# Tile norms' last steps and inverse roots on GpSimd instead of VectorE and ScalarE, in the second layer of a perceiver

## The chip, the cores and the metric

One core of a Trainium2 chip. The time is that of one whole execution on the device, in microseconds; lower is better. Engines are called TensorE (PE in the rows; PEld is its weight load), VectorE (DVE), ScalarE (ACT), GpSimd (POOL) and SyncE (SP). Each works through its own queue in program order and waits on semaphores.

## The reference

Two layers on latents x of 16 x 64 x 256 and a context of 16 x 1024 x 256. Each layer is cross-attention, then self-attention, then a feed-forward block, each behind a layer norm without weights and with a residual:

```python
def _layernorm(x, axis=-1, eps=1e-05):
    m = jnp.mean(x, axis=axis, keepdims=True)
    v = jnp.var(x, axis=axis, keepdims=True)
    return (x - m) / jnp.sqrt(v + eps)

x = x + _L1_xattn_ref(_layernorm(x, axis=-1), ctx_1024, ctx_1024, Wq, bq, Wk, bk, Wv, bv, Wo, bo)
x = x + _L1_attn_ref(_layernorm(x, axis=-1), Wq, Wk, Wv, W_O)
x = x + _L1_ffn_ref(_layernorm(x, axis=-1), w_gate, w_up, w_down)
```

The feed-forward block rounds its input to blockwise fp4, which are the steps that the change calls x steps:

```python
scale = jnp.max(jnp.abs(xb), axis=-1, keepdims=True) / 6.0
scale = jnp.maximum(scale, jnp.float32(1e-12))
xn = xb / scale
idx = jnp.searchsorted(_MID, jnp.abs(xn))
q = _GRID[idx] * jnp.sign(xn) * scale
```

## The kernel before

Everything is float32 and the order on each engine is written out by hand. The latents are 8 tiles of 128 rows (two batches) by 256. The first layer, its attention and its feed-forward block are not touched. The second layer (`second_layer`) is one program: a loop of 64 steps s, four for each of 16 batches, does the cross-attention, and the causal attention and the feed-forward block of finished tiles are woven into it. A tile is finished every 8 steps; `tile_at(s, lag)` says which tile has its turn in step s at a lag, and in this text the *place* of a step is (s - 10) mod 8, so that lag 12 falls at place 4 and lag 14 at place 6.

In a step the cross-attention does: TensorE `scores` (L722), in even steps `times_v` (L749) of a finished pair, `project_v` two steps ahead (L681), `transposes` of the step before in two halves (L732) and in between `project_k` four steps ahead (L667), unless that batch's keys were made early (batches 0, 4, 8, 12, 13 and 14: steps 12 to 15, 28 to 31 and 44 to 55 have no key projection, nor have the last four). VectorE takes two row maxima of 128x1024 (L859), an inverse of a row sum (L892), v out of its bank (L841), the transposed probabilities of one half (L869), the second inverse. ScalarE does two exponentials (L802) and takes the other half (L813) and the keys (L772). GpSimd multiplies the two halves of probabilities with the inverses (`normalise`, L655, 128x1024 each), twice in eight steps spreads the queries (L638), and for the causal attention does `spread_queries` (L1908, place 4) and `distances` (L1915, place 6). TensorE's results go round over banks 4 to 7, so TensorE waits for VectorE or ScalarE to empty a bank before it fills the next.

A tile norm (`TileNorm`; norm1 in front of the causal attention, tiles `ca_sn_*`; norm2 in front of the feed-forward block, tiles `ca_fn_*`) has four parts: statistics and variance on VectorE (L1698 to L1702; norm1 at place 0, norm2 at place 2), the root on ScalarE (L1706; norm1 at place 1, norm2 at place 4), and on VectorE a reciprocal, one Newton step (L1710 to L1717) and the 128x256 result (L1719; norm1 at place 2, norm2 at place 6). Square root and exponential are in different activation tables, so a table load stands before the root and one before the exponential after it. TensorE transposes norm1's result at place 3 (L1761), behind `project_v` and in front of that step's `transposes`.

Norm2's result goes through the x steps of the feed-forward input on VectorE: scale and division at place 6 (L173 to L176 on `ca_ff_x`), rounding at place 7 (L178 to L181 and L2069; scratch in `wi_gateT`). TensorE transposes it at place 0 (L1983). Behind the loop stands the tail (from 1299 us): the last two causal tiles and the feed-forward block's matmuls of all tiles (L1993, L2015), with rounding of the hidden values on VectorE and GpSimd. The norms of tile 7 (both) and 6 (norm2) fall in the tail, and so do the x steps of tiles 5 to 7.

## Time and profile before

| | us |
|---|---|
| three timed runs, median (lowest to highest) | 1418.12 (1415.79 to 1420.81) |
| the profiled execution | 1421.31 |
| its span, first to last instruction | 1418.0 |
| busy: TensorE matmuls | 1294.1 (91%) |
| busy: VectorE | 976.0 (69%) |
| busy: ScalarE | 802.0 (57%) |
| busy: GpSimd | 690.7 (49%) |

The profile is of one execution. A matmul's end is modelled, so TensorE can be shown as busy while it waits inside a group; how long a step takes is the surer figure. Idle time in brackets is that of the engine just before the instruction, with what ended it. The granted clock is TensorE's, 1.0 for 2.4 GHz and 0.5 for 1.2 GHz. An average over the span says little here, since the stages have different limits; what is to be read are the steps of the second layer's loop, from 725.8 to 1299 us.

### The profile page before, as it was taken

Reading aid. Unit: us, or ns where it says so; the run is one execution under the profiler, and the core shown is the slowest. Engines: PE = TensorE matmul, PEld = TensorE weight load, DVE = VectorE, ACT = ScalarE, POOL = GpSimd, SP = SyncE. Lnnn points to the kernel's source line nnn. Section 1 sums busy time; section 2 is a strip of 40 time slices with the busy share of each in tenths; the row PEclk is TensorE's granted clock in tenths of the full one; section 3 lists DMA queues with packets and bytes.
Section 4 is the critical chain, followed back from the end, with each engine's and each line's share of the span. In section 5 each row is a group of like instructions: output and inputs, shape, how many; then the busy total and the mean of one; then the engine's idle time right before and its main releaser. Section 6 shows DMA issues by size and latency. Waiting matters only on the chain. (4 is left out here: it accounts for less than half of the span.)

```text
span 1418.0 us, 28592 instructions
## 1 busy us (share of the span) xinstructions
PE 1294.1 (91%) x11120; PEld 899.6 (63%) x11122; DVE 976.0 (69%) x1876; ACT 802.0 (57%) x1373; POOL 690.7 (49%) x383
## 2 busy tenths in 40 slices
PE   6999999999999988988789999998998988888887
PEld 3666666667667665546456676666665676666564
DVE  4685776766666654856777767688766879776674
ACT  4766666666666655536456656556465645565431
POOL 2856656566666542310146654444445455544333
PEclk9999999999999999999999999999899989999999
DMA  5312112112113030007330210020010121000000
GB/s 164 101 51 66 46 46 67 46 60 76 46 46 113 2 113 1 1 5 219 106 93 31 60 52 31 31 61 31 31 51 31 44 61 47 31 2 1 5 9 18
DMA packets 30533, 74.23 MB, mean 52 GB/s; under 512 B 4033, under 2 KB 16193, under 8 KB 26177
## 3 DMA queue, kind: packets, MB, share of 16 engines
q1 hardware_dynamic: 30400, 72.41, 16.8%
q8 instruction: 90, 1.47, 0.4%
q14 instruction: 43, 0.34, 0.1%
HBM read 65.06 MB, written 7.34 MB: 51 GB/s over the span
## 5 line engine op out<-in xcount | busy, mean ns | idle before, releaser
L655 POOL TENSOR_TENSOR ca_prob<-ca_prob,ca_inv_sum 128x1024 f32<-128x1024 f32 x256 | 493.6, 1935 | 448.5 <-DVE ca_inv_sum L892 448.4
L732 PEld LDWEIGHTS bank<-ident,ca_prob 128*128 128x128 f32 x2048 | 240.9, 143 | 102.5 <-issue 75.2
L732 PE MATMUL bank<-ident,ca_prob 128*128 128x128 f32 x2048 | 273.7, 278 | 29.2 <-DVE ca_v L841 25.4
L856 DVE CUSTOM_DVE_ANT_0 ca_neg_logit<-bank,ca_mask_add 128x1024 f32<-128x1024 f32 x128 | 151.6, 1221 | 103.7 <-PE bank L722 76.6
L802 ACT ACTIVATE ca_prob<-bank,ca_neg_max 128x1024 f32<-128x1024 f32 x128 | 142.3, 1113 | 110.7 <-DVE ca_neg_max L859 110.5
L859 DVE TENSOR_REDUCE ca_neg_max<-bank 128x1 f32<-128x1024 f32 x128 | 150.5, 1218 | 59.9 <-PE bank L722 59.6
L802 ACT ACTIVATE ca_prob<-ca_neg_logit,ca_neg_max 128x1024 f32<-128x1024 f32 x128 | 146.9, 1149 | 68.3 <-DVE ca_neg_max L856 68.3
L869 DVE COPY ca_probT<-bank 128x512 f32<-128x512 f32 x256 | 163.7, 681 | 7.0 <-PE bank L732 7.0
L813 ACT ACTIVATE ca_probT<-bank 128x512 f32<-128x512 f32 x256 | 139.6, 594 | 50.8 <-PE bank L732 48.5
L722 PE MATMUL bank<-ca_kT,ca_q_blk 32*128 32x512 f32 x1024 | 150.3, 657 | 4.5 <-DVE ca_v L841 2.7
L749 PEld LDWEIGHTS bank<-ca_probT,ca_v 128*32 128x32 f32 x4096 | 111.8, 113 | 55.7 <-issue 42.4
L772 ACT ACTIVATE ca_kT<-bank,ca_bk 64x512 f32<-64x512 f32 x128 | 87.3, 682 | 104.1 <-PE bank L667 103.2
L749 PE MATMUL bank<-ca_probT,ca_v 128*32 128x128 f32 x4096 | 129.5, 280 | 4.9 <-issue 4.0
L667 PE MATMUL bank<-ca_ctxT,ca_wk 128*128 128x512 f32 x256 | 121.8, 601 | 10.1 <-DMA ca_bk<-in_L_xattn_bk 9.1
L681 PE MATMUL bank<-wv,ctxT 128*128 128x256 f32 x512 | 127.3, 392 | 0.0
L681 PE MATMUL bank<-ca_wv,ca_ctxT 128*128 128x256 f32 x512 | 127.3, 392 | 0.0
L681 PEld LDWEIGHTS bank<-ca_wv,ca_ctxT 128*128 128x128 f32 x512 | 92.3, 190 | 41.1 <-issue 28.2
L681 PEld LDWEIGHTS bank<-wv,ctxT 128*128 128x128 f32 x512 | 92.3, 190 | 41.2 <-issue 31.2
L772 ACT ACTIVATE ca_kT<-bank,ek_bk 64x512 f32<-64x512 f32 x80 | 54.6, 682 | 77.0 <-PE bank L667 76.3
L667 PE MATMUL bank<-ctxT,ek_wk 128*128 128x512 f32 x160 | 79.5, 624 | 4.4 <-DVE ca_v L841 2.4
L667 PEld LDWEIGHTS bank<-ca_ctxT,ca_wk 128*128 128x128 f32 x256 | 44.6, 193 | 43.6 <-issue 33.3
L892 DVE RECIPROCAL ca_inv_sum<-ca_row_sum 128x1 f32<-128x1 f32 x256 | 40.6, 159 | 41.6 <-ACT ca_prob L802 34.4
(281 smaller groups left out, 1712.2 us busy)
## 6 DMA issues: line engine op xcount, KB each, us to landing
ca_ctxT<-in_ctxT SPq DMA_DIRECT2D x16, 1024.0 KB, 5.3
ctxT<-in_ctxT SPq DMA_DIRECT2D x16, 1024.0 KB, 4.8
ca_mask_i<-in_mask SPq DMA_DIRECT2D x32, 256.0 KB, 6.1
ek_ctxT<-in_ctxT SPq DMA_DIRECT2D x12, 512.0 KB, 5.3
early_k<-ek_out SPq DMA_DIRECT2D x48, 128.0 KB, 3.4
ca_kT<-early_k SPq DMA_DIRECT2D x12, 512.0 KB, 5.7
...
```

The source lines that it names most:

```text
L655: pool.tensor_tensor(self.prob[:, x, :], self.prob[:, x, :], self.inv_sum[:, x:x + 1].broadcast_to([P, CTX]), ALU.mult).then_inc(self.norm ...
L667: mm = pe.matmul(self.core.bank[:, x, :], self.wk[:, k, m * P:(m + 1) * P], self.ctxT[:, b % 2, k, half * HALF_CTX:(half + 1) * HALF_CTX], ...
L681: mm = pe.matmul(self.core.bank[:, x, r * D:(r + 1) * D], self.ctxT[:, b % 2, k, ch * P:(ch + 1) * P], self.wv[:, k, :], start=(k == 0), s ...
L722: mm = pe.matmul(self.core.bank[:, 2 * j + half, :], self.q_blk[rows, b % 2, u, :, :], self.kT[rows, b % 2, u, :], start=True, stop=True, ...
L732: tr = pe.transpose(self.core.bank[:, x, n * P:(n + 1) * P], self.prob[:, 2 * (s % 2) + p, (4 * h + n) * P:(4 * h + n + 1) * P], self.core ...
L749: mm = pe.matmul(self.core.bank[32 * j:32 * j + 32, x, 0:P], self.v[:, b % 2, ch, m * P + 32 * j:m * P + 32 * j + 32], self.probT[:, n % 2 ...
L772: op = act.activation(self.kT[half * S:(half + 1) * S, b % 2, 2 * m + r, :], self.core.bank[r * S:(r + 1) * S, x, :], ACT.Identity, bias=s ...
L802: act.activation(self.prob[:, y, :], source, ACT.Exp, bias=self.neg_max[:, y:y + 1], scale=-1.0 if self.masked else 1.0, accum_out=self.ro ...
L813: self.banks.free(act.activation(self.probT[:, n % 2, 4 * h:4 * h + 4, 2 * (s % 2) + p, :], self.core.bank[:, x, :].rearrange("p (n q) -> ...
L856: dve.tensor_tensor_reduce(self.neg_logit[:, p, :], scores, self.mask_add[:, b % 2, :], -1.0, BIG, ALU.add, ALU.min, self.neg_max[:, y:y + ...
L859: dve.tensor_reduce(self.neg_max[:, y:y + 1], scores, AX.X, ALU.max, negate=True).then_inc(self.max_ready, 1)
L869: self.banks.free(dve.tensor_copy(self.probT[:, n % 2, 4 * h:4 * h + 4, 2 * (s % 2) + p, :], self.core.bank[:, x, :].rearrange("p (n q) -> ...
```

## The change

The square root on ScalarE is gone from the tile norms. VectorE makes a first guess of 1/sqrt(var) from the bits of the float (`first_guess`, two operations of 128x1), and three Newton steps of four 128x1 operations each (`improve`) make it exact enough. For the 7 first norms and the 6 second norms in the loop `improve` and the two 128x256 operations behind it (`finish_on_pool`: subtract the mean, multiply by the inverse root) run on GpSimd, norm1 at place 2 and norm2 at place 5, both behind that step's `normalise`. Norm2 was finished at place 6 before. In the tail, `improve` runs on VectorE.

Of the x steps, VectorE keeps the scale (0 to 2) at place 6 and one of the rounding operations (4) at place 7. GpSimd does the division (3, place 6), three operations at place 7 (5 to 7; the former `scalar_tensor_tensor` is a `tensor_scalar` and a `tensor_tensor`) and two at place 0 (8 and 9). TensorE transposes the result at place 1 instead of 0, and ScalarE takes it there. Statistics of a tile now wait until the norm of the tile before is finished. In the tail, TensorE's `times_v(30)` comes in front of the first gate projection, VectorE copies the last probabilities before it turns to the hidden values, and the x steps of tile 5 are shared with GpSimd.

```diff
+GUESS = 0x5F3759DF
 class TileNorm:
+    STEPS = 14
     def stats_on_vector(self, dve, t):
+        wait(dve, self.xn_ready, t)
...
-    def root_on_scalar(self, act, t):
-        act.wait_ge(self.var_ready, t + 1)
-        act.activation(self.std[:, :], self.var[:, :], ACT.Sqrt).then_inc(self.std_ready, 1)
+    def first_guess(self, dve, t):
+        bits = self.rstd[:, :].bitcast(I32)
+        dve.wait_ge(self.var_ready, t + 1)
+        dve.tensor_scalar(bits, self.var[:, :].bitcast(I32), 1, None, ALU.logical_shift_right).then_inc(self.fix_step, 1)
+        dve.wait_ge(self.fix_step, self.STEPS * t + 1)
+        dve.tensor_scalar(bits, bits, -1, GUESS, ALU.mult, ALU.add).then_inc(self.fix_step, 1)
+
+    def improve(self, eng, t):
+        done, n0 = self.fix_step, self.STEPS * t + 2
+        for n in range(n0, n0 + 12, 4):
+            eng.wait_ge(done, n)
+            eng.tensor_tensor(self.fix[:, :], self.rstd[:, :], self.rstd[:, :], ALU.mult).then_inc(done, 1)
+            eng.wait_ge(done, n + 1)
+            eng.tensor_tensor(self.fix[:, :], self.fix[:, :], self.var[:, :], ALU.mult).then_inc(done, 1)
+            eng.wait_ge(done, n + 2)
+            eng.tensor_scalar(self.fix[:, :], self.fix[:, :], -0.5, 1.5, ALU.mult, ALU.add).then_inc(done, 1)
+            eng.wait_ge(done, n + 3)
+            eng.tensor_tensor(self.rstd[:, :], self.rstd[:, :], self.fix[:, :], ALU.mult).then_inc(done, 1)
+        eng.wait_ge(done, n0 + 12)
+
+    def finish_on_pool(self, pool, t):
+        lat, wide = self.core.lat[:, t, :], [P, D]
+        self.improve(pool, t)
+        pool.tensor_tensor(self.xn[:, :], lat, self.mv[:, 0:1].broadcast_to(wide), ALU.subtract).then_inc(self.centred, 1)
+        pool.wait_ge(self.centred, t + 1)
+        pool.tensor_tensor(self.xn[:, :], self.xn[:, :], self.rstd[:, 0:1].broadcast_to(wide), ALU.mult)\
+            .then_inc(self.xn_ready, 1)
...
         @block.tensor
...
-                for t in tile_at(s, 16):
+                for t in tile_at(s, 17):
                     ff.latent_transposes(pe, t)
...
+            ca.times_v(pe, 30)
             ff.project(pe, 0, 0)
-            ca.times_v(pe, 30)
...
         @block.gpsimd
...
                 for t in tile_at(s, 6):
                     sa.distances(pool, t)
+                for t in tile_at(s, 2):
+                    causal_input(t)
+                for t in tile_at(s, 13):
+                    feed_forward_input(t)
+                for t in tile_at(s, 14):
+                    ff.x_step_on(pool, t, 3, 4)
+                for t in tile_at(s, 15):
+                    ff.x_step_on(pool, t, 5, 8)
+                for t in tile_at(s, 16):
+                    ff.x_step_on(pool, t, 8, 10)
...
         @block.vector
...
                 for t in tile_at(s, 2):
-                    causal_input(t)
+                    norm1.first_guess(dve, t)
+                for t in tile_at(s, 13):
+                    norm2.first_guess(dve, t)
...
                 for t in tile_at(s, 14):
-                    feed_forward_input(t)
+                    ff.scale_x(dve, t, norm2.xn_ready)
                 for t in tile_at(s, 15):
-                    ff.round_x(dve, t)
+                    ff.x_step_on(dve, t, 4, 5)
...
             ca.take_pv(dve, 30)
-            feed_forward_input(5)
+            ff.scale_x(dve, 5, norm2.xn_ready)
+            ca.take_t_on_vector(dve, STEPS - 1, 0)
             ff.hidden(dve, 0)
-            ff.round_x(dve, 5)
-            ca.take_t_on_vector(dve, STEPS - 1, 0)
             ff.round_hidden(dve, 0)
```

ScalarE's queue at the first norm of tile 0 (place 1 to 3; `ca_sn_std` is the root), one piece of the difference:

```order
 L813 ACTIVATE ca_probT<-bank 128x4x128 x2
-L1706 ACT_TABLE_LOAD
-L1706 ACTIVATE ca_sn_std<-ca_sn_var 128x1
-L802 ACT_TABLE_LOAD
 L802 ACTIVATE ca_prob,ca_row_sum<-bank,ca_neg_max 128x1024 x2
 L813 ACTIVATE ca_probT<-bank 128x4x128 x2
```

The root and both table loads are gone; the exponentials follow the copies at once. There are 634 rows of ScalarE before and 587 now.

VectorE's queue at places 6 and 7 of one tile, before (from the second inverse of place 6 to the maxima of the step behind place 7; `wi_gateT` is scratch):

```order
L892 RECIPROCAL ca_inv_sum<-ca_row_sum 128x1
L1710 RECIPROCAL ca_fn_rstd<-ca_fn_std 128x1
L1712 SCALAR_TENSOR_TENSOR ca_fn_fix<-ca_fn_rstd,ca_fn_var 128x1
L1715 TENSOR_SCALAR ca_fn_fix<-ca_fn_fix 128x1
L1717 TENSOR_TENSOR ca_fn_rstd<-ca_fn_rstd,ca_fn_fix 128x1
L1719 TENSOR_SCALAR ca_ff_x<-lat,ca_fn_mv,ca_fn_rstd 128x256
L173 TENSOR_REDUCE ca_ff_xmag<-ca_ff_x 128x16
L174 TENSOR_SCALAR ca_ff_xscale<-ca_ff_xmag 128x16
L175 RECIPROCAL ca_ff_xinv<-ca_ff_xscale 128x16
L176 TENSOR_TENSOR ca_ff_x<-ca_ff_x,ca_ff_xinv 128x256
L859 TENSOR_REDUCE ca_neg_max<-bank 128x1 x2
```

and now, of another tile:

```order
L892 RECIPROCAL ca_inv_sum<-ca_row_sum 128x1
L173 TENSOR_REDUCE ca_ff_xmag<-ca_ff_x 128x16
L174 TENSOR_SCALAR ca_ff_xscale<-ca_ff_xmag 128x16
L175 RECIPROCAL ca_ff_xinv<-ca_ff_xscale 128x16
L859 TENSOR_REDUCE ca_neg_max<-bank 128x1 x2
```

Six of the nine operations between the second inverse of place 6 and the next step's maxima have left VectorE.

GpSimd's queue from place 4 to place 7 of one tile, before:

```order
L1908 TENSOR_TENSOR ek_ctxT<-ek_ctxT,small 128x1024
L655 TENSOR_TENSOR ca_prob<-ca_prob,ca_inv_sum 128x1024 x4
L1915 TENSOR_TENSOR ek_out<-ek_out,ca_sa_top 128x1024
L655 TENSOR_TENSOR ca_prob<-ca_prob,ca_inv_sum 128x1024 x4
L638 TENSOR_TENSOR ca_q_blk<-ca_q,small 128x512
```

and now (two more rounds of the four 128x1 operations are left out):

```order
L655 TENSOR_TENSOR ca_prob<-ca_prob,ca_inv_sum 128x1024 x2
L1723 TENSOR_TENSOR ca_fn_fix<-ca_fn_rstd 128x1
L1725 TENSOR_TENSOR ca_fn_fix<-ca_fn_fix,ca_fn_var 128x1
L1727 TENSOR_SCALAR ca_fn_fix<-ca_fn_fix 128x1
L1729 TENSOR_TENSOR ca_fn_rstd<-ca_fn_rstd,ca_fn_fix 128x1
...
L1735 TENSOR_TENSOR ca_ff_x<-lat,ca_fn_mv 128x256
L1737 TENSOR_TENSOR ca_ff_x<-ca_ff_x,ca_fn_rstd 128x256
L655 TENSOR_TENSOR ca_prob<-ca_prob,ca_inv_sum 128x1024 x2
L1938 TENSOR_TENSOR ek_out<-ek_out,ca_sa_top 128x1024
L176 TENSOR_TENSOR ca_ff_x<-ca_ff_x,ca_ff_xinv 128x256
```

Between the products of place 5 and those of place 6 there now stand 14 operations, and the division stands behind the distances. At place 2 the same 14 stand on `ca_sn_*` and `ek_ctxT`. GpSimd has 188 rows in all before and 421 now.

## Rows read from the trace of the kernel before

**Rows 1.** windows, first without norm, then place 6: us; each engine's busy us; PEclk

```profile
776.52:784.86 8.34, 8.34 (x101) 5.96 (x97) 6.62 (x10) 4.78 (x10) 5.09 (x3) 1.00 0.01 2
...
1082.58:1094.13 11.55, 11.55 (x118) 8.66 (x115) 10.43 (x18) 5.34 (x10) 5.65 (x3) 1.00 0.09 13
...
sum 66.64, PE 64.89 PEld 49.21 DVE 58.75 ACT 28.43 POOL 33.32; mean PE 10.81 PEld 8.20 DVE 9.79 ACT 4.74 POOL 5.55
```

**Rows 2.** windows of place 5: without root, with one, and the sum of six

```profile
833.15:841.39 8.24, 7.40 (x88) 5.92 (x92) 6.82 (x10) 3.42 (x6) 7.22 (x5) 1.00 0.28 89
903.12:917.90 14.78, 11.96 (x73) 8.12 (x76) 6.90 (x10) 8.09 (x13) 7.48 (x5) 0.77 0.01 2
...
sum 68.98, PE 55.63 PEld 40.75 DVE 41.28 ACT 36.21 POOL 47.49; mean PE 9.27 PEld 6.79 DVE 6.88 ACT 6.04 POOL 7.92
```

**Rows 3.** windows of places 7 and 0: before feed-forward input, and sum of six

```profile
849.23:867.35 18.12, 17.89 (x213) 12.53 (x214) 12.20 (x22) 12.74 (x23) 9.85 (x6) 1.00 0.17 60
...
sum 116.22, PE 102.23 PEld 68.25 DVE 84.84 ACT 73.46 POOL 51.78; mean PE 17.04 PEld 11.38 DVE 14.14 ACT 12.24 POOL 8.63
```

**Rows 4.** timeline of ScalarE in step 39: start us, us, instruction

```profile
1069.99 1.28 ACT L1706 ACT_TABLE_LOAD   x1
...
1071.51 1.28 ACT L802 ACT_TABLE_LOAD   x1
```

**Rows 5.** timeline of TensorE in steps 39 to 41; in brackets idle before

```profile
1074.96 2.00 PE L1792 MATMUL bank<-ek_ctxT 64*128 64x64 f32 x32 [2.83 <-DVE ca_v L841]
1076.89 3.66 PE L667 MATMUL bank<-ctxT,ek_wk 128*128 128x512 f32 x4
...
1087.04 1.88 PE L667 MATMUL bank<-ctxT,ek_wk 128*128 128x512 f32 x4
...
1089.72 1.14 PE L722 MATMUL bank<-ca_kT,ca_q_blk 32*128 32x512 f32 x8
...
1092.62 1.04 PE L732 MATMUL bank<-ident,ca_prob 128*128 128x128 f32 x8
```

**Rows 6.** timeline of VectorE in step 40

```profile
1088.48 1.89 DVE L1712 SCALAR_TENSOR_TENSOR ca_fn_fix<-ca_fn_rstd,ca_fn_var 128x1 f32<-128x1 f32 x1
...
1090.60 1.64 DVE L1717 TENSOR_TENSOR ca_fn_rstd<-ca_fn_rstd,ca_fn_fix 128x1 f32<-128x1 f32 x1
...
1094.13 2.35 DVE L859 TENSOR_REDUCE ca_neg_max<-bank 128x1 f32<-128x1024 f32 x2
```

**Rows 7.** timeline of GpSimd in step 40

```profile
1085.33 1.89 POOL L655 TENSOR_TENSOR ca_prob<-ca_prob,ca_inv_sum 128x1024 f32<-128x1024 f32 x1 [7.27 <-DVE ca_inv_sum L892]
1088.47 1.89 POOL L655 TENSOR_TENSOR ca_prob<-ca_prob,ca_inv_sum 128x1024 f32<-128x1024 f32 x1 [1.25 <-DVE ca_inv_sum L892]
1090.32 1.90 POOL L1915 TENSOR_TENSOR ek_out<-ek_out,ca_sa_top 128x1024 f32<-128x1024 f32 x1
```

**Rows 8.** timeline of TensorE in steps 13, 36 and 37

```profile
820.32 1.46 PE L732 MATMUL bank<-ident,ca_prob 128*128 128x128 f32 x8 [1.95 <-DVE ca_v L841]
...
1046.44 2.00 PE L1843 MATMUL bank<-ek_ctxT 64*64 64x256 f32 x16 [0.85 <-DVE ca_attnT L883]
...
1054.07 0.38 PE L1761 MATMUL bank<-ident,ek_ctxT 128*128 128x128 f32 x2
```

**Rows 9.** timeline of GpSimd at the start and in step 36

```profile
0.24 0.10 POOL L2544 MEMSET const-float32-0.0<- 128x1 f32 x1 [0.24 <-issue]
...
1048.24 1.89 POOL L655 TENSOR_TENSOR ca_prob<-ca_prob,ca_inv_sum 128x1024 f32<-128x1024 f32 x1 [0.52 <-DVE ca_inv_sum L892]
```

**Rows 10.** groups of GpSimd by form: count, busy us, mean ns, idle before

```profile
L638 POOL TENSOR_TENSOR ca_q_blk<-ca_q,small 128x512 f32<-128x512 f32 x32 | 33.2, 1038 | 43.0 <-DVE ca_q L832 43.0
```

**Rows 11.** timeline of TensorE in the tail

```profile
1316.84 3.64 PE L749 MATMUL bank<-ca_probT,ca_v 128*32 128x128 f32 x64 [4.04 <-issue]
...
1387.54 0.61 PE L1983 MATMUL bank<-ident,ca_ff_x 128*128 128x128 f32 x2 [2.92 <-DVE ca_ff_x L2069]
```

More of the change, by code:

```diff
@@ L2043, in take_hidden, with x_free, x_step_on, scale_x @@
                         ("fh", t, 1))
-    def x_free(self, dve, t):
+    def x_free(self, eng, t):
         if t >= 1:
-            self.banks.wait_filled(dve, ("fx", t - 1))
-    def x_steps(self):
-        return fp4_steps(self.x[:, :], DB, self.xmag[:, :], self.xscale[:, :], self.xinv[:, :], self.x[:, :],
-                         self.xe)
-    def divide_x(self, dve, t, xn_ready):
-        dve.wait_ge(xn_ready, t + 1)
-        steps = self.x_steps()
-        for n in range(4):
-            steps[n](dve).then_inc(self.x_step, 1)
-            dve.wait_ge(self.x_step, 8 * t + n + 1)
-    def round_x(self, dve, t):
-        steps = self.x_steps()
-        for n in range(4, 8):
-            steps[n](dve).then_inc(self.x_step, 1)
-            dve.wait_ge(self.x_step, 8 * t + n + 1)
-        grid, scale = fp4_scaled(self.x[:, :], self.xscale[:, :], DB)
-        dve.tensor_tensor(grid, grid, scale, ALU.mult).then_inc(self.x_ready, 1)
+            self.banks.wait_filled(eng, ("fx", t - 1))
+    def x_step_on(self, eng, t, first, last):
+        x, e = self.x[:, :], self.xe
+        steps = fp4_steps(x, DB, self.xmag[:, :], self.xscale[:, :], self.xinv[:, :], x, e)
+        grid, scale = fp4_scaled(x, self.xscale[:, :], DB)
+        for n in range(first, last):
+            wait(eng, self.x_step, 9 * t + n)
+            if n < 6:
+                steps[n](eng).then_inc(self.x_step, 1)
+            elif n == 6:
+                eng.tensor_scalar(x, x, 1.0 - 2.0**-24, None, ALU.mult).then_inc(self.x_step, 1)
+            elif n == 7:
+                eng.tensor_tensor(x, x, e, ALU.add).then_inc(self.x_step, 1)
+            elif n == 8:
+                steps[7](eng).then_inc(self.x_step, 1)
+            else:
+                eng.tensor_tensor(grid, grid, scale, ALU.mult).then_inc(self.x_ready, 1)
+    def scale_x(self, dve, t, xn_ready):
+        dve.wait_ge(xn_ready, t + 1)
+        self.x_step_on(dve, t, 0, 3)
     def h_steps(self, t):
@@ L2320, in _ @@
                     sa.take_heads(act, t)
-                for t in tile_at(s, 16):
+                for t in tile_at(s, 17):
                     ff.take_latents(act, t)
@@ L2331, in _ @@
                     ca.take_q_on_scalar(act, 1)
-                for t in tile_at(s, 1):
-                    norm1.root_on_scalar(act, t)
                 for t in tile_at(s, 3):
@@ L2338, in _ @@
                     sa.take_transposed(act, t)
-                for t in tile_at(s, 12):
-                    norm2.root_on_scalar(act, t)
             ff.silu(act, 0)
@@ L2443, in _ @@
             ff.round_hidden(dve, 1)
-            causal_input(7)
+            norm1.first_guess(dve, 7)
+            banks.wait_filled(dve, ("sx", 6))
+            norm1.finish_on_vector(dve, 7)
             ff.hidden(dve, 2)
@@ L2455, in _ @@
             ff.hidden(dve, 4)
-            ff.round_x(dve, 6)
+            ff.x_step_on(dve, 6, 4, 10)
             sa.divide(dve, 7)
```

41 lines of the change are left out of this document (19 added, 22 removed).

## The prediction

> **What bounds the kernel now.** I read the windows first, one for each step of the second layer's cross-attention loop (64 steps, from 725.8 to 1299 us of the span; a step begins with VectorE's first row maximum), because the change touches this loop and the tail behind it and nothing before them. Then I read who waits inside the long steps.
>
> The loop repeats every 8 steps with one latent tile. Step s has place (s - 10) mod 8. At place 6, a step without any norm takes 8.34 us and TensorE is busy in all of it; the same TensorE work takes 11.55 as soon as VectorE also has the last steps of the second norm in it, and VectorE is then busy for 10.43 [rows 1]. Place 5 takes up to 14.78 us with a second norm's root in front of it and 8.24 without [rows 2]. Places 7 and 0 together take 18.12 us before there is feed-forward input, and (116.22 - 18.12) / 5 = 19.6 on average in the next five pairs [rows 3]. So the loop is TensorE's by nature, and some 8 to 10 us in every 8 steps go to other engines at three places.
>
> What they are is seen in one tile. *Place 5, ScalarE:* the root costs two table loads of 1.28 us, the second charged to the next exponential, which so can't begin before 1072.79 [rows 4]; without them it could begin with its maximum, at about 1070.6. VectorE's take of v comes behind its inverse, and so behind that exponential; TensorE waits 2.83 us for it, and then the granted clock falls: the key projection takes 3.66 us there and 1.88 in the next step [rows 5], and the mean clock of the worst step at this place is 0.77 [rows 2], a mix of the 2.4 and the 1.2 GHz level. *Place 6, VectorE:* a 128x1 operation with two SBUF inputs takes 1.89 us, exactly until GpSimd's 128x1024 multiply ends, and the next such takes 1.64, until GpSimd's next operation ends [rows 6, 7]. The scores of step 41 are complete at 1090.86 [rows 5] and their maximum starts at 1094.13 [rows 6].
>
> **The change part by part.** All sums are made against the profiled execution: 1421.3 us with a span of 1418.0, 3.2 above the median of the three timed runs (1418.1).
>
> *1. Place 6, norm off VectorE.* Five long steps, 66.64 - 8.34 = 58.3 us [rows 1]. From the end of the second blocked operation to the maximum there are 1.9 us (1092.24 to 1094.13 [rows 6]) for five operations, three of which stay: under 1.2 us, and the short step leaves VectorE 8.34 - 6.62 = 1.7 [rows 1]. Four steps go to 8.34. The fifth, step 48, has no key projection and is bound by VectorE: I put it at 8.1. New sum 41.5, gain **16.8**.
>
> *2. Place 5, no table loads.* Five steps, 68.98 - 8.24 = 60.7 us [rows 2]. The 8.24 us step has no key projection, like three of the five; with 0.35 for two new 128x1 operations (first_guess) those come to 8.6. The other two have one: 8.24 less the 0.84 that TensorE was idle in it, plus 1.88 [rows 2, 5], is 9.3; since part of those 8.24 was VectorE's, I take 9.0. New sum 43.8, gain 16.9. If the idle went but the low clock stayed, only the wait would be won, some 2.3 us in each, 11.5 in all. Step 63 has the same stall in front of the tail: 1.5 more. Together **18.4**.
>
> *3. Places 7 and 0.* 98.1 us in five pairs [rows 3]. VectorE keeps one of five rounding operations, and TensorE no longer starts place 7 behind a late maximum. At 18.12 each the sum is 90.6; one pair has no key projections and may get 2 more. Gain **9.5**, between nothing and that.
>
> *4. Places 2 and 3, the first norm.* Its table loads end in a wait of TensorE, 0.85 us in front of the causal output [rows 8], seven tiles: 6.0. Against it stands a new latency: GpSimd does 12 operations of 128x1 and two of 128x256 behind its normalise. Their price is in no row. From 128x512 in 1.04 [rows 10] and 128x1024 in 1.89 [rows 7] the fixed part is 1.04 - 0.85 = 0.19, and a memset of 128x1 takes 0.10 [rows 9]. Between 0.10 and 1.04 I take 0.25 with the hand-over, nearest to the fixed part: 12 x 0.25 = 3.0. A 128x256 is 0.19 + 0.43 = 0.62, two are 1.3. So x is ready 4.3 us behind the normalise. TensorE left 3.9 in step 36 (1050.13 to 1054.07 [rows 8, 9]): short by 0.4. In the four tiles without key projections TensorE comes 1.9 sooner: short by 2.3, but there it waited 1.95 just behind these transposes [rows 8]. At worst 3 x 0.4 + 4 x 2.3 = 10.4 lost; with that wait and an exponential that starts sooner I take 3. Net **3**.
>
> *5. What GpSimd's queue does to others.* Behind the 4.3 us stands the next step's normalise. At place 5 GpSimd has 3.8 + 4.3 = 8.1 of 8.6 us; but TensorE reads the product only in the step after: one normalise ends at 1087.2 [rows 7], its transposes start at 1092.6 [rows 5], 5 us later, and a delay of 1 to 2 hides in that. Places 6, 7 and 0 get about 0.6, 2.4 and 1.4 us more. I cost it at nothing; the cover is that slack, and beyond it each microsecond costs one per step. VectorE loses a little: at place 7 its one rounding operation may meet a busy GpSimd for up to 1.9 us, five times, mostly in slack: **-2.5**.
>
> The page "SBUF — State Buffer" of the Trainium skill (Who interferes with whom) says that a VectorE operation with two SBUF inputs and a GpSimd operation that reads SBUF exclude each other for a whole instruction; the 1.89 and 1.64 above agree. By it everything moved to GpSimd is one more thing to wait for, but what stays of the norms on VectorE in the loop has one SBUF input, so it leaves the sum as it is.
>
> *6. The tail.* TensorE waits 4.04 us in front of the last times_v [rows 11], for copies that VectorE makes behind the rounding of x(5); the new order puts the copy first and the rounding on GpSimd: -4. The norms of tiles 7, 6 and 7 stay on VectorE, with 14 small operations instead of 4; at about 0.19 each 10 more cost 1.9, part of which lies in waits like those of rows 6. The last stands in front of a wait of TensorE, 2.92 us for x(7) [rows 11], and costs its full 1.9 with the one more rounding operation; the two others together 1. Net -4 + 2.9: a gain of **1**, between 6 and -3.
>
> Sum: 16.8 + 18.4 + 9.5 + 3 - 2.5 + 1 = 46 us. 1421.3 - 46 = 1375, and as a median 3 below that: **1372 us**.
>
> **The rivals.**
>
> *GpSimd's small operations are dear (the other side).* Place: the 14 GpSimd operations between the normalise and TensorE's transposes of x at place 3, which in TensorE's order stand before everything else of that step. Each 0.1 us above 0.25 adds 1.2 us to seven first norms, 8.4 in all. Above about 0.5 the second norm fills place 5 too (3.8 + 6 + 1.3 over 8.6), 12 us per tile for each further microsecond. At 0.5: 21 us lost, 1393. The gain is used up at about 0.7; at 0.75 the first norms lose 12 x 0.5 x 7 = 42 and the second 12 x 0.25 x 6 = 18, 60 against 46 won: 1432. Against it: the fixed part of 0.19. For it: no row shows a 128x1 arithmetic operation on GpSimd. The page "GPSIMD Engine Reference" of the Trainium skill (Performance versus the Vector engine) keeps elementwise work on VectorE, with 1.96 times its time for an addition of 2048 elements; that speaks against the change only where GpSimd becomes the bound, and no row here shows that.
>
> *The low clock moves with the idle.* TensorE idles some 2 us in front of x at place 3 in four tiles, and the half-clock stretches stay. Then term 2 keeps 11.5 of 16.9, term 3 about 3 of 9.5, and term 4 is -1: 46 - 15.9 = 30 us, 1388.
>
> *More than forecast.* VectorE doesn't bound the steps without key projection, which drop by up to 1.9 at five places, and the tail gives 6: 46 + 9 + 5 = 60 us, 1358.
>
> *The waits were hidden anyway,* and something that I don't see sets the step: 1418. Against it: 8.34 against 11.55 us at equal TensorE work.
>
> **How the numbers follow.** Forecast (1362 to 1382) 0.50; more than that 0.15; low clock stays, or small operations at 0.4 to 0.5 (1382 to 1400) 0.25; dear operations short of break-even 0.05; no change 0.02; slower 0.03. The range leaves out the far end of the 0.15 and the last three: 1354 to 1398. Faster by over 0.3% (about what a measurement of this kernel can tell) 0.95, within it 0.02, slower by over 0.3% 0.03.
>
> **What would show it.** Step 40 at 8.3 to 8.5 us, step 39 at about 9; no table load between the first step and the tail; GpSimd's 128x1 operations 0.25 us from start to start; TensorE's idle in front of the transposes of x at place 3 under 1 us with key projection and 2 to 3 without; the granted clock 1.0 at places 5 and 7. The forecast is wrong if the 128x1 operations take 0.5 or more, or if TensorE waits for a normalise that stands behind them.

## The result

The changed kernel takes 1378.74 us (median of 4 runs, 1377.42 to 1384.67), the kernel before 1416.95 beside it (1411.2 to 1420.81): ratio 0.9742, 95% interval 0.9697 to 0.9786, some 37 us less. The forecast was 1372 in 1354 to 1398. The profiled executions took 1377.42 and 1421.31 us, with spans of 1375.6 and 1418.0. The first is the fastest of the changed kernel's four and the second slower than all four of the other's, so the differences between the two traces add up to 42.4 us, some 5 more than the ratio gives. Of the other kernels below, only the profiled execution of roots ran at a lower mean clock than its timed ones (0.923 against 0.975; 1429.31 us), so only its times are used.

The head of the page of the changed kernel: VectorE and ScalarE are each busy for some 40 us less, GpSimd for 74 more, with 601 instructions where the kernel before had 383 (the counts under The change are of merged rows).

```profile
span 1375.6 us, 28748 instructions
PE 1270.7 (92%) x11120; PEld 881.9 (64%) x11122; DVE 935.1 (68%) x1839; ACT 759.8 (55%) x1326; POOL 764.6 (56%) x601
```

The loop of the second layer, up to the first maximum of its last step 63, went from 566.6 to 521.5 us; what is left, step 63 and the tail, from 125.6 to 129.2. TensorE's mean granted clock rose from 0.95 to 0.99 in the first stretch and was 0.90 and 0.89 in the second. Windows of the changed kernel (columns as in [rows 1]): place 6 without norm, then with one and the sum of six, against [rows 1]; place 5 in step 31 and the sum, against [rows 2]; places 7 and 0, the sum, against [rows 3].

```profile
775.66:784.00 8.34, 8.34 (x101) 5.96 (x97) 6.62 (x10) 4.78 (x10) 5.09 (x3) 1.00 0.00 0
1057.95:1066.30 8.35, 8.35 (x101) 5.96 (x97) 7.21 (x13) 4.79 (x10) 5.82 (x7) 1.00 0.01 2
sum 49.66, PE 49.66 PEld 36.17 DVE 42.60 ACT 26.36 POOL 39.42; mean PE 8.28 PEld 6.03 DVE 7.10 ACT 4.39 POOL 6.57
...
972.83:984.64 11.81, 8.81 (x67) 7.07 (x68) 7.10 (x13) 3.53 (x6) 10.83 (x18) 0.71 0.01 1
sum 56.75, PE 48.40 PEld 37.07 DVE 42.23 ACT 23.93 POOL 52.19; mean PE 8.07 PEld 6.18 DVE 7.04 ACT 3.99 POOL 8.70
...
sum 109.19, PE 105.51 PEld 74.09 DVE 72.71 ACT 74.69 POOL 79.64; mean PE 17.58 PEld 12.35 DVE 12.12 ACT 12.45 POOL 13.27
```

Place 6 now takes as long as a step without norm. Place 5 is shorter except in step 31, which keeps its 12 us and its low clock.

Timeline of TensorE in step 39 and GpSimd at its end (start, duration, instruction, idle before in brackets). Where TensorE waited 2.83 us and then ran at half clock [rows 5] it waits 0.69 and keeps its clock (1.98 us for the key projection), and GpSimd's 128x1 operation takes 0.19 us, 0.27 from start to start.

```profile
1052.03 2.00 PE L1815 MATMUL bank<-ek_ctxT 64*128 64x64 f32 x32 [0.69 <-DVE ca_v L841]
1053.96 1.98 PE L667 MATMUL bank<-ctxT,ek_wk 128*128 128x512 f32 x4
...
1055.08 0.19 POOL L1723 TENSOR_TENSOR ca_fn_fix<-ca_fn_rstd 128x1 f32<-128x1 f32 x1
1055.35 0.19 POOL L1725 TENSOR_TENSOR ca_fn_fix<-ca_fn_fix,ca_fn_var 128x1 f32<-128x1 f32 x1
```

In the tail small operations of the first norm of tile 7 stand still on VectorE while GpSimd works, and TensorE waits for the norm (5.40 us; before 2.5). TensorE also waits longer in front of L1866, for a causal result that VectorE makes behind the second norm of tile 6, and in front of L2006, for x(7): 4.85 us each, where it was 3.1 and 2.92 [rows 11].

```profile
1279.60 1.28 DVE L1723 TENSOR_TENSOR ca_sn_fix<-ca_sn_rstd 128x1 f32<-128x1 f32 x1
1280.92 0.16 DVE L1725 TENSOR_TENSOR ca_sn_fix<-ca_sn_fix,ca_sn_var 128x1 f32<-128x1 f32 x1
1281.11 0.15 DVE L1727 TENSOR_SCALAR ca_sn_fix<-ca_sn_fix 128x1 f32<-128x1 f32 x1
1281.30 1.04 DVE L1729 TENSOR_TENSOR ca_sn_rstd<-ca_sn_rstd,ca_sn_fix 128x1 f32<-128x1 f32 x1
...
1284.75 0.69 PE L1784 MATMUL bank<-ident,ek_ctxT 128*128 128x128 f32 x2 [5.40 <-DVE ek_ctxT L1742]
```

The same norm's operations stood still in the kernel before, too, and for as long in all (2.4 us):

```profile
1330.35 1.54 DVE L1712 SCALAR_TENSOR_TENSOR ca_sn_fix<-ca_sn_rstd,ca_sn_var 128x1 f32<-128x1 f32 x1
...
1332.10 1.24 DVE L1717 TENSOR_TENSOR ca_sn_rstd<-ca_sn_rstd,ca_sn_fix 128x1 f32<-128x1 f32 x1
```

What is new there is their number: from the first of them to the start of the 128x256 operation it is 5.13 us now and was 3.23.

### The profile page after: what moved, and what is told of

It reads as the page before. It is cut to its first block and busy times, and to the rows that moved or that the text cites. A ratio compares the mean times of both kernels' runs of the same rounds, so it can differ in the third digit from the quotient of the medians.

```text
span 1375.6 us, 28748 instructions
## 1 busy us (share of the span) xinstructions
PE 1270.7 (92%) x11120; PEld 881.9 (64%) x11122; DVE 935.1 (68%) x1839; ACT 759.8 (55%) x1326; POOL 764.6 (56%) x601
## 5 line engine op out<-in xcount | busy, mean ns | idle before, releaser
L732 PEld LDWEIGHTS bank<-ident,ca_prob 128*128 128x128 f32 x2048 | 237.2, 142 | 76.2 <-issue 53.3
L732 PE MATMUL bank<-ident,ca_prob 128*128 128x128 f32 x2048 | 267.1, 275 | 7.3 <-DVE ca_v L841 4.3
L722 PE MATMUL bank<-ca_kT,ca_q_blk 32*128 32x512 f32 x1024 | 147.2, 644 | 4.6 <-DVE ca_v L841 2.7
L749 PEld LDWEIGHTS bank<-ca_probT,ca_v 128*32 128x32 f32 x4096 | 108.7, 110 | 48.7 <-issue 33.4
L749 PE MATMUL bank<-ca_probT,ca_v 128*32 128x128 f32 x4096 | 126.0, 275 | 0.9 <-DVE ca_probT L869 0.9
L667 PE MATMUL bank<-ctxT,ek_wk 128*128 128x512 f32 x160 | 76.0, 600 | 2.6 <-PEq L100 2.1
L722 PEld LDWEIGHTS bank<-ca_kT,ca_q_blk 32*128 32x128 f32 x1024 | 40.4, 184 | 30.7 <-issue 26.0
```

The source lines that it names most:

```text
L667: mm = pe.matmul(self.core.bank[:, x, :], self.wk[:, k, m * P:(m + 1) * P], self.ctxT[:, b % 2, k, half * HALF_CTX:(half + 1) * HALF_CTX], ...
L722: mm = pe.matmul(self.core.bank[:, 2 * j + half, :], self.q_blk[rows, b % 2, u, :, :], self.kT[rows, b % 2, u, :], start=True, stop=True, ...
L732: tr = pe.transpose(self.core.bank[:, x, n * P:(n + 1) * P], self.prob[:, 2 * (s % 2) + p, (4 * h + n) * P:(4 * h + n + 1) * P], self.core ...
L749: mm = pe.matmul(self.core.bank[32 * j:32 * j + 32, x, 0:P], self.v[:, b % 2, ch, m * P + 32 * j:m * P + 32 * j + 32], self.probT[:, n % 2 ...
```

## The experiments

The change does three things at once: no square root on ScalarE, the norms' last steps on GpSimd, and the rounding of x on GpSimd. My theory was that the first pays at places 5, 2 and 3, and the second at place 6, because GpSimd makes VectorE's operations with two SBUF inputs stand still there. The rivals were that only one of the two matters, or that it is the number of VectorE's operations that counts. Ratios are to the kernel before, run on the same chip; 0.001 is 1.4 us.

| kernel | median us | ratio | 95% interval |
|---|---|---|---|
| the change | 1378.74 | 0.9742 | 0.9697 to 0.9786 |
| roots | 1397.45 | 0.9852 | 0.9815 to 0.9889 |
| root2 | 1386.44 | 0.9781 | 0.9745 to 0.9818 |
| vector_norms | 1422.28 | 1.0045 | 1.0027 to 1.0063 |
| vector_singles | 1383.11 | 0.9765 | 0.9722 to 0.9808 |
| before_singles | 1393.38 | 0.9843 | 0.9811 to 0.9875 |
| x_vector | 1391.64 | 0.9801 | 0.9752 to 0.9850 |
| pool_long1 | 1405.94 | 0.9936 | 0.9913 to 0.9960 |
| pool_singles | 1376.55 | 0.9708 | 0.9674 to 0.9742 |
| fw_late | 1377.82 | 0.9735 | 0.9707 to 0.9762 |
| swap | 1375.44 | 0.9706 | 0.9676 to 0.9736 |
| tail_singles | 1376.15 | 0.9714 | 0.9687 to 0.9741 |
| best | 1356.79 | 0.9590 | 0.9566 to 0.9615 |

### The square roots back: roots, root2

```diff
                 if s == Q_STEPS[0]:
                     ca.take_q_on_scalar(act, 1)
+                for t in tile_at(s, 1):
+                    norm1.root_on_scalar(act, t)
...
+                for t in tile_at(s, 12):
+                    norm2.root_on_scalar(act, t)
```

> The changed kernel with ScalarE's square roots back in the loop of the second layer, at their old places 1 and 4, on the same variance; nobody uses the result (only the next tile's variance waits for it). Norms and rounding stay where the change put them. Theory (the table loads are what place 5 and places 2 and 3 paid for, VectorE's blocked operations are a second cause at place 6): the exponential of place 5 is late again by 1.28 + 1.28 us, TensorE waits and the granted clock falls there; of the 12.3 us won at place 5 nearly all is lost again and of the 11.1 at places 2 and 3 about 7: 1379 + 19 = 1398 us, 1391 to 1402. Place 6 stays at 8.3 to 8.8. Rival (the gain is VectorE's relief alone, ScalarE has room for its tables): within 3 us of 1379.

Measured 1397.45, as the theory had it; where in the loop it was lost isn't shown. root2 has the second norm's root alone:

> The changed kernel with ScalarE's square root back for the second norm only, at place 4 of the loop (unused result, as in the run that brought both back). Theory (the table loads at place 5 alone carry term 2): place 5 goes from 56.8 us in its six steps back to 69, as before the change, places 2 and 3 stay: 1379 + 12 = 1391 us, 1388 to 1394; the other 7 of the 18.7 us that both roots cost belong to the first norm's. Rival (it is the first norm's root that costs): 1379 to 1384.

Measured 1386.44: 7.7 us for the second norm's root, not 12, and 18.7 - 7.7 = 11.0 for the first norm's (by the ratios 5.5 and 10). Its place 5 takes 65.9 us instead of 56.8; in step 39 the stall is what it was in [rows 4, 5], with the half clock behind it:

```profile
1055.68 1.28 ACT L802 ACT_TABLE_LOAD   x1
...
1059.13 3.68 PE L1821 MATMUL bank<-ek_ctxT 64*128 64x64 f32 x32 [2.83 <-DVE ca_v L841]
```

The roots thus cost 16 us by the ratios (19 by the medians) in the changed kernel, where nobody reads their result; what they cost the kernel before, which needs it, no run shows.

### The norms on VectorE again, in two forms: vector_norms, vector_singles

```diff
                 for t in tile_at(s, 14):
+                    norm2.first_guess(dve, t)
+                    ff.x_free(dve, t)
+                    norm2.finish_on_vector(dve, t)
                     ff.scale_x(dve, t, norm2.xn_ready)
```

(The first norm gets the same at place 2, and GpSimd keeps the second norm of tile 5 alone.)

> The changed kernel with the Newton steps and the last step of both norms on VectorE in the loop, at the places of the kernel before (tile 5's second norm, in the last step of the loop, stays on GpSimd). No table loads come back; each norm has nine 128x1 operations with two SBUF inputs on VectorE, where the kernel before had two. Theory (such an operation waits for the end of GpSimd's, up to 1.9 us each): place 6 goes from 8.3 back over 11.5 us, to 12 to 15, and place 2 gets longer too: 1379 + 5 x 4 to 5 x 7 + up to 10 = 1399 to 1424. Rival (only the table loads mattered, VectorE has 1.7 us to spare in that step): 1379 to 1384.

Measured 1422.28, 0.45% slower than the kernel before. VectorE and GpSimd in step 40:

```profile
1079.98 1.64 DVE L1723 TENSOR_TENSOR ca_fn_fix<-ca_fn_rstd 128x1 f32<-128x1 f32 x1
1081.65 1.83 DVE L1725 TENSOR_TENSOR ca_fn_fix<-ca_fn_fix,ca_fn_var 128x1 f32<-128x1 f32 x1
1083.51 0.15 DVE L1727 TENSOR_SCALAR ca_fn_fix<-ca_fn_fix 128x1 f32<-128x1 f32 x1
1083.70 0.16 DVE L1729 TENSOR_TENSOR ca_fn_rstd<-ca_fn_rstd,ca_fn_fix 128x1 f32<-128x1 f32 x1
...
1079.71 1.89 POOL L655 TENSOR_TENSOR ca_prob<-ca_prob,ca_inv_sum 128x1024 f32<-128x1024 f32 x1 [1.25 <-DVE ca_inv_sum L892]
1081.56 1.90 POOL L1938 TENSOR_TENSOR ek_out<-ek_out,ca_sa_top 128x1024 f32<-128x1024 f32 x1
```

The first two tensor_tensor operations end where GpSimd's two end (1081.6, 1083.5). From then on GpSimd is idle and the same operations take 0.16 us.

```diff
-            eng.tensor_tensor(self.fix[:, :], self.rstd[:, :], self.rstd[:, :], ALU.mult).then_inc(done, 1)
-            eng.tensor_tensor(self.fix[:, :], self.fix[:, :], self.var[:, :], ALU.mult).then_inc(done, 1)
+            eng.tensor_scalar(self.fix[:, :], self.rstd[:, :], self.rstd[:, 0:1], self.var[:, 0:1], ALU.mult,
+                              ALU.mult).then_inc(done, 1)
...
-            eng.tensor_tensor(self.rstd[:, :], self.rstd[:, :], self.fix[:, :], ALU.mult).then_inc(done, 1)
+            eng.tensor_scalar(self.rstd[:, :], self.rstd[:, :], self.fix[:, 0:1], None, ALU.mult).then_inc(done, 1)
```

> As vector_norms, but each Newton step is three tensor_scalar operations on 128x1 (the factors come in as the per-partition scalars), so none has two full SBUF inputs; 9 instead of 12 operations. Theory (it is the exclusion with GpSimd that costs, not the number of small operations): each takes about 0.1 us whatever GpSimd does, 9 x 0.1 to 9 x 0.15 = about 1.2 us per norm, inside the 1.7 us that VectorE is idle at place 6: 1376 to 1386 us, place 6 at 8.3 to 9. Rival (many small dependent operations on VectorE cost by their number): like vector_norms, over 1395.

Measured 1383.11, on the same engine and at the same places: 39 us less by the form (this includes the tail, which has the new form too, and nine operations for each norm instead of twelve). VectorE in step 40, with GpSimd busy from 1065.85 to 1069.60:

```profile
1066.87 0.27 DVE L1723 TENSOR_SCALAR ca_fn_fix<-ca_fn_rstd,ca_fn_var 128x1 f32<-128x1 f32 x1
1067.17 0.15 DVE L1726 TENSOR_SCALAR ca_fn_fix<-ca_fn_fix 128x1 f32<-128x1 f32 x1
1067.36 0.21 DVE L1728 TENSOR_SCALAR ca_fn_rstd<-ca_fn_rstd,ca_fn_fix 128x1 f32<-128x1 f32 x1
...
1068.36 1.40 DVE L1741 TENSOR_SCALAR ca_ff_x<-lat,ca_fn_mv,ca_fn_rstd 128x256 f32<-128x256 f32 x1
```

None of the nine small operations stands still. But the 128x256 one does, and place 6 takes 10.65 us, not the 8.3 to 9 that I expected.

### The form alone, in the kernel before: before_singles

```diff
-        dve.scalar_tensor_tensor(self.fix[:, :], self.rstd[:, :], self.rstd[:, 0:1], self.var[:, :], ALU.mult,
-                                 ALU.mult).then_inc(self.fix_step, 1)
+        dve.tensor_scalar(self.fix[:, :], self.rstd[:, :], self.rstd[:, 0:1], self.var[:, 0:1], ALU.mult,
+                          ALU.mult).then_inc(self.fix_step, 1)
...
-        dve.tensor_tensor(self.rstd[:, :], self.rstd[:, :], self.fix[:, :], ALU.mult).then_inc(self.fix_step, 1)
+        dve.tensor_scalar(self.rstd[:, :], self.rstd[:, :], self.fix[:, 0:1], None, ALU.mult).then_inc(self.fix_step, 1)
```

> The kernel before with two operations of each norm in another form: the 128x1 scalar_tensor_tensor and tensor_tensor of its Newton step become tensor_scalar with the factors as per-partition scalars. Same engine, same number, the square roots stay on ScalarE. Theory (the 1.89 and 1.64 us at place 6 are GpSimd's exclusion, which tensor_scalar of one element does not meet): these two drop to about 0.25 each, 3.0 us per norm; the 128x256 operations behind them are then met by GpSimd instead and give 1.2 to 1.5 back, so place 6 goes from 11.5 to about 9.9 in five steps: -8, and -3 in place 2 and the tail: 1416 - 11 = 1405, 1400 to 1409. Rival (what VectorE lacks at place 6 is time for all its operations): 1414 to 1416.

Measured 1393.38: 22 us gained where I expected 11, by two operations in another form, as many as before on the same engine. Between the two traces, 28.4 us apart, place 6 gives 6.3 us; places 2 and 3, which I had at 1 or 2, give 9.6, places 7 and 0 give 5.1, the tail 3.3. VectorE at place 6, against [rows 6]:

```profile
1074.24 0.27 DVE L1712 TENSOR_SCALAR ca_fn_fix<-ca_fn_rstd,ca_fn_var 128x1 f32<-128x1 f32 x1
1074.55 0.15 DVE L1715 TENSOR_SCALAR ca_fn_fix<-ca_fn_fix 128x1 f32<-128x1 f32 x1
1074.74 0.21 DVE L1717 TENSOR_SCALAR ca_fn_rstd<-ca_fn_rstd,ca_fn_fix 128x1 f32<-128x1 f32 x1
1074.99 1.28 DVE L1719 TENSOR_SCALAR ca_ff_x<-lat,ca_fn_mv,ca_fn_rstd 128x256 f32<-128x256 f32 x1
...
1076.76 1.30 DVE L174 TENSOR_SCALAR ca_ff_xscale<-ca_ff_xmag 128x16 f32<-128x16 f32 x1
```

22 us for the form and 16 for the roots make 38; the whole change gives 37. The first was measured in the kernel before and the second in the changed one, and no run has both with the rounding of x left on VectorE, so it isn't shown that they add up. What is shown is that moving the norms adds little once their form is right: vector_singles, with everything of the norms on VectorE, is within 5 us of the change, and 7 behind tail_singles, which shares its tail. Its rounding of x stands on GpSimd, as in the change; what that is worth comes next.

### The rounding of x on VectorE again: x_vector

```diff
                 for t in tile_at(s, 14):
                     ff.scale_x(dve, t, norm2.xn_ready)
+                    ff.x_step_on(dve, t, 3, 4)
                 for t in tile_at(s, 15):
-                    ff.x_step_on(dve, t, 4, 5)
+                    ff.x_step_on(dve, t, 4, 6)
+                    wait(dve, ff.x_step, 9 * t + 6)
+                    ff.x_both(dve)
+                    ff.x_step_on(dve, t, 8, 10)
```

(x_both is the scalar_tensor_tensor of the kernel before. GpSimd's three calls go, and TensorE and ScalarE turn to the result one step sooner.)

> The changed kernel with the rounding of the feed-forward input on VectorE in the loop, as before the change: its divide at place 6, the other five operations at place 7, TensorE's transposes of it at place 0 again in place of 1. The norms stay on GpSimd. Theory (term 3 of the sum): the 7.0 us that places 7 and 0 won are lost, place 6 gets some 1 us longer in one or two tiles, place 1 gives 2.0 back: 1379 + 5 = 1384, 1382 to 1389. Rival (VectorE has enough room without the norms; those places were won by TensorE not starting behind a late maximum): 1379 - 2 = 1377.

Measured 1391.64, 13 us more than the change by the medians and 8 by the ratios, more than expected, but not where expected. Place 1 gives its 2.0 us back (53.8 to 51.8). Place 7 loses 3.4 and place 0 wins 1.5, so places 7 and 0 lose 1.9 of the 7.0 us that I had put there; this speaks for the rival on the late maximum. The surprise is place 6, 57.5 to 66.2 in seven steps. (Place 5 takes 3.9 more with the same idle time in each step, by half clock alone; the four executions spread from 1381 to 1395.) Two operations stand still there in step 40:

```profile
1069.80 1.65 DVE L174 TENSOR_SCALAR ca_ff_xscale<-ca_ff_xmag 128x16 f32<-128x16 f32 x1
1071.49 0.25 DVE L175 RECIPROCAL ca_ff_xinv<-ca_ff_xscale 128x16 f32<-128x16 f32 x1
1071.77 1.79 DVE L176 TENSOR_TENSOR ca_ff_x<-ca_ff_x,ca_ff_xinv 128x256 f32<-128x256 f32 x1
```

In the changed kernel L174 stands still for 1.65 us as well, but it is the last that does, and the maximum is ready to start 0.25 us before its scores are there.

### What GpSimd's chain costs: pool_long1, pool_singles

```diff
-        for n in range(n0, n0 + 12, 4):
+        for n in range(n0, n0 + (self.STEPS - 2 if t < 7 else 12), 4):
```

(STEPS is 26 for the first norm and stays 14 for the second.)

> The changed kernel with six Newton steps instead of three in the first norm of tiles 0 to 6 on GpSimd (the extra steps change nothing in the result): 12 more dependent 128x1 operations at 0.26 to 0.27 us from start to start, 3.2 us. It measures what each further microsecond of this chain costs, the premise of the rival on dear operations. Theory (the chain already ends just behind what TensorE has to do in every tile, so nearly all of it shows): 7 x 3.2 = 22 us, less some slack in the three tiles with key projections: 1379 + 20 = 1399, 1396 to 1402. Rival (TensorE's work or later slack absorbs it): up to 1385.

Measured 1405.94, 27 us for 7 x 12 x 0.27 = 22.8 us more chain: 1.2 us for each. TensorE's idle in front of the transposes of x, from the line's view of the changed kernel (idle us, times):

```profile
  POOL ek_ctxT L1737: 9.3, 4
```

and of pool_long1:

```profile
  POOL ek_ctxT L1737: 32.6, 7
```

23.3 us more are idle; the rest is half clock behind it (granted clock 0.79 to 0.87 in five of the seven steps, 1.0 in all seven before). The chain was to be shortened by the new form:

> As tail_singles (which took 1376), and GpSimd's Newton steps in the loop are three tensor_scalar operations each too: 9 operations instead of 12. Theory (six Newton steps instead of three cost 30 us at place 3, 1.35 us for each of the chain): 3 x 0.27 = 0.8 us less per first norm, 7 x 0.8 to 7 x 0.8 x 1.4: 1376 - 7 = 1369, 1367 to 1372. Rival (a tensor_scalar with scalars from SBUF takes longer on GpSimd than the 0.19 us of the others, no row shows it): 1375 to 1378.

Measured 1376.55, the same as tail_singles; the rival holds. Its three operations on GpSimd (minimum/median/maximum ns) take 0.81 us together, the four of the change 0.76 with one more hand-over:

```profile
L1723 POOL TENSOR_SCALAR ca_sn_fix<-ca_sn_rstd,ca_sn_var x21: 340/341/342, 814.9 to 1239.9; 128x1 f32<-128x1 f32 x21
L1726 POOL TENSOR_SCALAR ca_sn_fix<-ca_sn_fix x21: 190/190/191, 815.3 to 1240.3; 128x1 f32<-128x1 f32 x21
L1728 POOL TENSOR_SCALAR ca_sn_rstd<-ca_sn_rstd,ca_sn_fix x21: 277/283/296, 815.6 to 1240.6; 128x1 f32<-128x1 f32 x21
```

### What is left at place 5: fw_late, swap

Step 31 was the one that won nothing. fw_late changes `FW_SCALE = (10, 31, 52)` to `(10, 32, 52)`.

> The changed kernel with GpSimd's scaling of the second feed-forward weight (2.8 us) one step later, in step 32 instead of 31. Theory (at place 5 GpSimd has normalise 3.8 + norm 4.3 + scaling 2.8 us = 10.9 in an 11.8 us step; that step alone of place 5 won nothing, 11.98 to 11.82): step 31 goes to 9.3 to 9.7 and step 32 stays near 8.3, 1379 - 2.3 = 1376.5 us. Rival (the stall of step 31 has another cause, or only moves): 1379 to 1380.

Measured 1377.82: my theory on the scaling fell. TensorE still waits 3.00 us. GpSimd, TensorE and VectorE of fw_late in steps 30 and 31:

```profile
972.14 3.33 POOL L655 TENSOR_TENSOR ca_prob<-ca_prob,ca_inv_sum 128x1024 f32<-128x1024 f32 x1 [0.52 <-DVE ca_inv_sum L892]
975.43 1.04 POOL L638 TENSOR_TENSOR ca_q_blk<-ca_q,small 128x512 f32<-128x512 f32 x1
976.43 1.89 POOL L1931 TENSOR_TENSOR ek_ctxT<-ek_ctxT,small 128x1024 f32<-128x1024 f32 x1
...
978.38 0.89 PE L1815 MATMUL bank<-ek_ctxT 64*128 64x64 f32 x12 [3.00 <-POOL ek_ctxT L1931]
...
971.98 1.74 DVE L181 TENSOR_TENSOR ca_fw_raw<-ca_fw_raw,ca_fw_e 128x1536 f32<-128x1536 f32 x1
```

This time VectorE stops GpSimd: its weight rounding started first, and GpSimd's normalise takes 3.33 us instead of 1.89. Behind it stand the next block of queries and the spread of the causal queries, for which TensorE waits. The kernel before has the same 3.33 and 3.00. swap puts the spread in front:

```diff
+                for t in tile_at(s, 4):
+                    sa.spread_queries(pool, t)
                 if s % GROUPS == 2 and s // GROUPS + 1 < B:
                     ca.queries(pool, s // GROUPS + 1)
-                for t in tile_at(s, 4):
-                    sa.spread_queries(pool, t)
```

> The changed kernel with GpSimd's spread of the causal queries (place 4) in front of its next block of cross-attention queries instead of behind it. The trace shows TensorE's causal scores at place 5 waiting for this spread in every tile (1.0 to 3.0 us, 3.0 in step 31, where VectorE's weight rounding also holds GpSimd up), while nobody needs the other block before the step's end. Theory (the stall left at place 5 is GpSimd's queue, not the norm's): each of six stalls shortens by up to 1.04 us, the half clock behind step 31's goes: 1379 - 6 = 1373, 1370 to 1376. Rival (the block of queries is needed at once, or the stall has another end): 1379 to 1382.

Measured 1375.44, 3 us less by the medians and 5 by the ratios; the intervals overlap, but the stall of step 31 is 2.00 us instead of 3.00 and place 5 takes 54.7 instead of 56.8. In steps 15, 23 and 55 the wait for the spread is gone, and one of 0.7 us for v stands there, as in step 39.

### The tail: tail_singles

The operations take the form of vector_singles, for the three norms in the tail only.

> The changed kernel, its loop untouched; in the tail alone the three norms that VectorE does there (first norm of tile 7, second of tiles 6 and 7) take each Newton step as three tensor_scalar operations instead of four operations of which three have two SBUF inputs. Theory (the tail lost 3.6 us instead of winning 1 because these small operations stand still while GpSimd works, and TensorE waits for each norm): the tail falls from 129.2 to the 118.9 us that it took in vector_singles: 1379 - 10 = 1369 us, 1366 to 1372. Rival (the tail is set by where the loop leaves it, the low clock ahead of it, and vector_singles came into it with other work done): 1379.

In the profile the tail takes 120.0 us instead of 129.2, and the first norm of tile 7, from its guess to its end, 3.3 instead of 5.5. But the profiled execution (1370.58) is the fastest of six; the median of 1376.15 is only 3 to 4 us better. The mean clock is 0.985 in that one and 0.978 to 0.981 in the others. Which stretches the other executions ran at half clock isn't recorded, so where some 5 us of the 9 went stays open.

### What the runs point to: best

All Newton steps in the new form, on VectorE, behind the guess and beside GpSimd's normalise; GpSimd keeps the two 128x256 operations.

```diff
     def finish_on_pool(self, pool, t):
         lat, wide = self.core.lat[:, t, :], [P, D]
-        self.improve(pool, t)
+        pool.wait_ge(self.fix_step, self.STEPS * (t + 1))
...
                 for t in tile_at(s, 2):
                     norm1.first_guess(dve, t)
+                    norm1.improve(dve, t)
                 for t in tile_at(s, 13):
                     norm2.first_guess(dve, t)
+                    norm2.improve(dve, t)
```

With it go swap and three moves in VectorE's tail: the first norm of tile 7 ahead of `ff.round_hidden(dve, 1)`, `sa.divide(dve, 7)` ahead of the rounding of x(6), and the rounding of x(7) ahead of `ff.round_hidden(dve, 5)`.

> What the runs so far point to, together. All Newton steps are three tensor_scalar operations, and VectorE does them, also in the loop, right behind the guess, while GpSimd is still at its normalise; GpSimd keeps the two 128x256 operations of each norm and the rounding. The spread of the causal queries stands in front of the next block of queries. In the tail the first norm of tile 7 stands in front of the rounding of hidden(1), the causal divide of tile 7 in front of the rounding of x(6), and the rounding of x(7) in front of that of hidden(5). Theory: the 12 x 0.27 = 3.2 us leave GpSimd's chain and GpSimd cannot stop them on VectorE: TensorE's idle at place 3 (0.15 to 3.44 us, 10.3 in seven tiles) nearly goes, -9, against +1 where VectorE has no room; the spread gives 3; the tail goes from 129 to 121 by the form of the operations and to 116 by its order, of which a half shows in the median if it is as with tail_singles: 1379 - 8 - 3 - 3 - 5 = 1360 us, 1354 to 1366. Rival (with 2 us more on VectorE at places 2 and 5 TensorE waits there for its maxima and the low clock returns): 1370 to 1375.

Measured 1356.79 (1354.79 to 1356.95), ratio 0.9590: 22 us better than the change, 56 than the kernel before. Windows of place 3, the sum of seven steps, for the change:

```profile
sum 64.92, PE 54.59 PEld 40.53 DVE 39.01 ACT 38.33 POOL 45.26; mean PE 7.80 PEld 5.79 DVE 5.57 ACT 5.48 POOL 6.47
```

and for best:

```profile
sum 57.70, PE 50.25 PEld 37.17 DVE 38.46 ACT 37.86 POOL 31.25; mean PE 7.18 PEld 5.31 DVE 5.49 ACT 5.41 POOL 4.46
```

Place 3 gives 7.2 us, place 2 takes 4.2 back, where VectorE has two us more to do: 3.0 net against the 8 that I had expected. Step 63 and the tail take 115.8 us instead of 129.2, 13.4 of the 20.7 us between the two spans. The granted clock is 1.00 in the whole loop. How the tail's 13.4 us divide between form and order isn't shown, since no run has the order alone; tail_singles, with the form alone, took 120.0.

## Why the prediction was right, and where not

The time was near (1378.7 against 1372, a gain of 37 us against 46) and the range held, but the terms were less good than their sum. By the two spans (1418.0 - 1375.6 = 42.4 us against 46):

| | forecast | measured |
|---|---|---|
| 1. place 6 | 16.8 | 17.0 |
| 2. place 5, step 63 | 18.4 | place 5: 12.2 |
| 3. places 7 and 0 | 9.5 | 7.0 |
| 4. places 2 and 3 | 3 | 11.0 |
| 5. GpSimd's queue | -2.5 | place 1: -2.0 |
| 6. tail | 1 | with step 63: -3.6 |
| rest | 0 | 0.8 |

**Term 1** was right: 66.64 to 49.66 us. Its margin was luck. I wrote that what stays of the norms on VectorE has one SBUF input and so leaves the sum as it is, and gave the three operations that stay of the x steps under 1.2 us. They took 2.4, since L174 (128x16) stood still for 1.65; 0.25 us of slack were left. The section that I had cited for two inputs ("SBUF — State Buffer" of the Trainium skill, Who interferes with whom) also counts a tensor_scalar in a 2-port mode among the operations that GpSimd excludes. The 128x16 and 128x256 ones here fit that. The 128x1 ones never stood still, which fits only if they run outside that mode, and no row here shows the mode. I had read half the rule.

**Term 2** was 6 us too large, and the step that failed is the first: I charged every long step at place 5 to the root, from one tile. One line's view of L1792 in the kernel before, which I had not read, tells who ended TensorE's waits there (us, times):

```profile
  POOL ek_ctxT L1908: 8.1, 4
  DVE ca_v L841: 7.6, 3
```

In the changed kernel the same view of L1815 says 10.0 us in six waits for the spread, 0.7 in one for v. The waits for v were the root's and went, but for the 0.7. Four of seven, step 31 and step 63 among them, were GpSimd's before and stayed, so that step 63's 1.5 us were not won. root2 says the same from the other side: 7.7 us for this root. Even of the 12.2 us, 2.1 are step 47's, which waits 1.89 us for the spread in both kernels and got shorter by its clock alone (0.75 to 1.00); in pool_singles it took 11.61 us again, at 0.73.

**Term 3** was near in size (116.22 to 109.19). Of its two reasons the rounding counts for less: x_vector loses only 1.9 us at places 7 and 0 without it, and before_singles wins 5.1 us there with all of it on VectorE.

**Term 4** was 8 us too small. The new latency was priced well: 0.27 us an operation where I took 0.25, TensorE's idle in front of x 1.8 to 3.4 us in four tiles and under 0.1 in three (forecast 2 to 3, and under 1). What failed is the gain: 0.85 us for each root, from one wait. It was 11.0 us for the seven (roots less root2), and the first norm's two-input operations on VectorE at place 2, which had no place in the term, gave 9.6 at places 2 and 3 in before_singles.

**Term 5** feared a late normalise behind the norm at place 5. It didn't show: steps 24, 32 and 40 take 8.34 or 8.35 us. What TensorE does wait for at place 5 is the spread, which stands ahead of the norm in GpSimd's queue; in four steps the change left that wait as it was. Place 1's 2.0 us, for TensorE's transposes of x that moved there, were in no term.

**Term 6** had the copy in front of times_v right (its wait is gone), and the price of the norms nearly: 1.9 us more for each, and the three took 1.9, 2.8 and 1.7 more up to the 128x256 operation, with no more standing still in the first than before. What failed is the slack. I gave the first two 1 us together and the third its full 1.9, but TensorE's waits for the three grew by 2.9, 1.7 and 1.9 us, 6.5 in all.

**The rivals.** "Dear operations" had its slope: pool_long1 gives 1.2 us for each us of chain, so an operation at about 0.65 us would have used up the gain by the first norms alone (an estimate: 37 us / (7 x 12 x 1.2) = 0.37 above 0.27), where I said 0.7. "Low clock moves with the idle" did not come true: the granted clock is 1.00 at place 3 in all seven tiles, with up to 3.4 us of idle in front of x. It stayed low in step 31 (0.71 before and now), whose idle stayed too, and in the tail (0.90 and 0.89). "More than forecast" and "hidden anyway" fell with the time.
